# A five-layer attention stack on one core: the softmax shifts as eight rows per group, and who carries them

## What is computed

```
x = L0(x)                     # a0: cross attention on the normalised context
x = L1(x)                     # s1: self attention; c1: cross attention, raw context; m1: MLP
x = L2(x)                     # s2: self attention; c2: cross attention, normalised context; m2: MLP
x = L3(x)                     # l3: attention on the context with one wide head, experts, gate
attn = softmax(einsum('bhnd,bhsd->bhns', q, k) * HD ** -0.5)   # N = 256 queries, S = 1601 keys (or 256)
o = einsum('bhns,bhsd->bhnd', attn, v)
```

## Time and profile before

| what | value |
|---|---|
| median of the runs | 6120.44 us |
| the profiled execution: its own time | 6116.53 us |
| its span, first to last instruction | 6114.7 us |
| TensorE busy | 5496.7 us (90%) |
| ScalarE busy | 4374.0 us (72%) |
| VectorE busy | 4071.9 us (67%) |
| GpSimd busy | 990.6 us (16%) |
| mean granted TensorE clock | 0.976 |

### The profile page before, as it was taken

How to read it: one execution, slowest core, us unless ns; L and a number is a source line. 1 busy time by engine, 2 the same in 40 slices (tenths; PEclk the granted TensorE clock), 3 DMA queues, 4 the chain that set the end, 5 groups by cost and what they waited for, 6 DMA issues and landing times.

```text
span 6114.7 us, 229584 instructions
## 1 busy us (share of the span) xinstructions
PE 5496.7 (90%) x101728; PEld 3464.1 (57%) x101728; DVE 4071.9 (67%) x6107; ACT 4374.0 (72%) x8158; POOL 990.6 (16%) x1660
## 2 busy tenths in 40 slices
PE   5999999999877899999999977789999999998998
PEld 3555555656444466666666444446666666655665
DVE  5777777777555677777777445567777777744443
ACT  3888887888666688888888656568888888863333
POOL 3122122121111111111111011112211221200000
PEclk9999999999999899999999989989999999999999
DMA  2222222222112222222222011122222222211110
GB/s 94 83 78 60 85 75 61 87 74 59 49 56 65 86 74 74 78 85 75 77 74 82 2 58 58 59 86 81 64 78 87 75 65 85 75 44 33 46 59 27
DMA packets 230104, 414.47 MB, mean 68 GB/s; under 512 B 23904, under 2 KB 131472, under 8 KB 228624
## 3 DMA queue, kind: packets, MB, share of 16 engines
q1 hardware_dynamic: 229136, 400.04, 21.9%
HBM read 316.81 MB, written 83.14 MB: 65 GB/s over the span
## 4 chain that ended last, share of the span: by engine, by line
PE 66%; ACT 13%; DVE 9%; issue 5%; DMA 3%; POOL 2%; SPq 1%; ACTq 0%; DVEq 0%; POOLq 0%
PE bank L1158 25%; PE bank L1279 14%; PE pair L1158 14%; ACT P L1426 6%; DVE MX L1589 5%; ACT KSF L1396 2%; PE bank L758 2%; PE bank L749 1%; ACT QP L1364 1%; PE pair L685 1%; DMA QP<-scr_q 1%; PE bank L1195 1%; DMA scr_ks<-KSF 1%; ACT REST L1397 1%; PE pair L522 1%
## 5 line engine op out<-in xcount | busy, mean ns | idle before, releaser
L1589 DVE TENSOR_REDUCE MX<-pair 128x2 f32<-128x802 f32 x3072 | 2985.9, 990 | 1043.2 <-PE pair L1158 1030.6
L1426 ACT ACTIVATE P<-bank 128x512 f32<-128x512 f32 (+1 forms) x5504 | 3183.3, 597 | 606.3 <-PE bank L1158 497.6
L1158 PE MATMUL bank<-QP,KP 128*32 128x256 bf16 (+2 forms) x40192 | 2260.7, 274 | 223.7 <-ACT P L1426 169.7
L1158 PE MATMUL pair<-KP,QP 96*32 96x401 bf16 (+2 forms) x25264 | 1837.8, 335 | 152.9 <-DMA QP<-scr_q 98.9
L1158 PEld LDWEIGHTS bank<-QP,KP 128*32 128x32 bf16 (+2 forms) x40192 | 1109.0, 96 | 1356.6 <-ACT P L1426 345.3
L1279 PE MATMUL bank<-P,VA 128*25 128x256 f32 (+1 forms) x22016 | 1737.6, 383 | 0.5 <-ACT P L1426 0.5
L1158 PEld LDWEIGHTS pair<-KP,QP 96*32 96x32 bf16 (+1 forms) x25264 | 773.3, 97 | 297.6 <-DVE MX L1589 140.2
L1279 PEld LDWEIGHTS bank<-P,VA 128*25 128x25 f32 (+1 forms) x22016 | 641.3, 104 | 136.3 <-issue 47.1
L1718 POOL COPY VA<-VN 128x416 f32<-128x416 f32 (+1 forms) x320 | 139.7, 437 | 2745.8 <-PE bank L1279 1529.6
L1593 DVE TENSOR_REDUCE MX<-pair 128x4 f32<-128x1024 f32 x256 | 312.0, 1223 | 343.2 <-PE pair L1158 342.2
L1698 POOL TENSOR_TENSOR REST<-REST,KSF 128x401 f32<-128x401 f32 (+1 forms) x224 | 203.7, 910 | 538.0 <-ACT REST L1397 538.0
(11 more groups left out here) (245 smaller groups left out, 4235.7 us busy)
## 6 DMA issues: line engine op xcount, KB each, us to landing
KP<-scr_k SPq DMA_DIRECT2D x768, 225.1 KB
QP<-scr_q SPq DMA_DIRECT2D x960, 48.0 KB
CN<-ctx_n SPq DMA_DIRECT2D x40, 768.0 KB
scr_k<-KSF SPq DMA_DIRECT2D x48, 600.8 KB, 3.4
scr_k<-KSF SPq DMA_DIRECT2D x48, 600.0 KB, 3.3
CT<-ctx_t SPq DMA_DIRECT2D x24, 800.5 KB, 4.4
KP<-scr_ks SPq DMA_DIRECT2D x128, 144.0 KB
scr_q<-QS SPq DMA_DIRECT2D x80, 192.0 KB, 2.1
```

Of the source, the lines that this page charges most:

```text
L1158: last = nc.tensor.matmul(out[c:c + m, :], lhsT[:, c:c + m], rhs, start=start, stop=stop)
L1426: nc.scalar.activation(P[v % 2][0:kt, half * 2 * N:(half + 1) * 2 * N], SC[half][0:kt, :], ACT.Exp, scale=SCALE).then_inc(sem("probs_full" ...
L1589: nc.vector.tensor_reduce(MX[:, r, c:c + 2], MP[j % 2][:, :].rearrange("p (t k) -> p t k", t=2)[:, :, 0:SPANS[0][1]], AX.X, ALU.max).then_ ...
```

## The change

- **Rows.** NMB becomes 2 x 24 columns (query half, then 8 columns of shifts with zeros on both sides). `shifts` writes the 4 heads x (high, low) side by side. TensorE's 8 products become 2, each with 16 columns of weights (`row_products`): the result is 16 partitions x 256 queries, of which 8 carry one head's high and low each.
- **Ones per head.** Rows 96 to 111 of KP are one only in the columns of the head that a row belongs to, and zero elsewhere (`head_rows`). All four heads share the same 16 rows of QP.
- **Who copies.** VectorE copies the 16 x 256 to QP for the first head, waits for itself, and spreads it from SBUF to SBUF over the three others (16 x 768). ScalarE's two copies are gone. Both halves of tile 0's scores wait for the spread.
- **Self attentions.** The same from MP[1]; TensorE's `maximum` 1 of the next group waits for the copy (`rows_copied`), no longer for both of ScalarE's. Columns of MP are ordered by query half first.
- **Statistics.** `bn_aggr` of tile t - 1 stands behind `bn_stats` of tile t; the last slot has two.
- **Start.** VectorE's 2 memsets of rows become 32 (GpSimd's too); two small ones clear NMB.

```diff
+def head_rows():
+    cross, own = [(h, h * S, (h + 1) * S) for h in range(1, G)], [(h, h * N, (h + 1) * N) for h in range(G)]
+    return [[(2 * h + 2, c0, c1, 1.0) for h, c0, c1 in cross] + [(2, G * N, S, 1.0)] +
+            [(8 + 2 * h + 2, c0, c1, 1.0) for h, c0, c1 in own],
+            [(2 * h, c0, c1, 0.0) for h, c0, c1 in cross] + [(8 + 2 * h, c0, c1, 0.0) for h, c0, c1 in own],
+            [(2, 0, G * N, 1.0)]]
...
# tensor: piece "rows", and shift_rows with MP[1] and rows_full
-                    for half in range(2):
-                        for r in range(4):
-                            last = nc.tensor.matmul(MISC[ROWS_AT[half]:ROWS_AT[half] + 2, r * 128:(r + 1) * 128],
-                                                    NMB[g % 2][:, 4 * half + r, :], IDB[:, :], start=True, stop=True)
-                    last.then_inc(sem("misc_full"), 1)
+                    row_products(ph, g, MISC).then_inc(sem("misc_full"), 1)
...
+            def row_products(ph, g, out):
+                c = 8 if ph.cross else 0
+                for qt in range(2):
+                    last = nc.tensor.matmul(out[MR:MR + NR, qt * 128:(qt + 1) * 128], NMB[g % 2][:, qt, c:c + NR],
+                                            IDB[:, :], start=True, stop=True)
+                return last
...
# tensor: scores, t == 0
-                    use, pair = rows_at[ph.name, b, g]
-                    if use is not None and half:
-                        pe.wait_ge(sem("misc_free"), use + 1)
-                    else:
-                        pe.wait_ge(sem("rows_done"), pair + half + 1)
+                    pe.wait_ge(sem("rows_done"), rows_at[ph.name, b, g] + 1)
...
# tensor: maximum, j == 1
-                    pe.wait_ge(sem("rows_done"), rows_before(ph, b, g)[1] + 2)
+                    pe.wait_ge(sem("rows_copied"), rows_before(ph, b, g) + 1)
...
# scalar: piece "rows" (copy_rows in the self attentions goes alike)
-                    act.wait_ge(sem("misc_full"), el.use(role, "r" + name[-1]) + 1)
-                    nc.scalar.copy(QP[g][MR:MR + 2, half * 2 * N:(half + 1) * 2 * N],
-                                   MISC[ROWS_AT[half]:ROWS_AT[half] + 2, :]).then_inc(
-                        sem("misc_free" if half else "rows_done"), 1)
...
# vector: start
-            dve.wait_ge(sem("keys_cleared"), 1)
-            for g in range(2):
-                last = nc.vector.memset(KP[g][MR:MR + 2, :], 1.0)
-            last.then_inc(sem("packs_set"), 1)
+            for k, step in enumerate(head_rows()):
+                dve.wait_ge(sem("keys_cleared"), k + 1)
+                for g in range(2):
+                    for rows, c0, c1, value in step:
+                        last = nc.vector.memset(KP[g][MR:MR + rows, c0:c1], value)
+                last.then_inc(sem("keys_cleared"), 1)
...
# vector: rows
+            def spread_rows(g):
+                nc.vector.tensor_copy(QP[g][MR:MR + NR, N:G * N].rearrange("p (h q) -> p h q", q=N),
+                                      QP[g][MR:MR + NR, 0:N].unsqueeze(1).to_broadcast([NR, G - 1, N])).then_inc(
+                    sem("rows_done"), 1)
...
                 if role == "rows":
+                    use, g = el.use(role, name), el.group(int(name[1]) + 1)[2]
+                    dve.wait_ge(sem("misc_full"), use + 1)
+                    nc.vector.tensor_copy(QP[g][MR:MR + NR, 0:N], MISC[MR:MR + NR, 0:N]).then_inc(sem("misc_free"), 1)
+                    dve.wait_ge(sem("misc_free"), use + 1)
+                    spread_rows(g)
                     return
...
# vector: statistics
-                    wait_apart(dve, "stats_read", at("stats_read", b, t + 1))
-                    last = nc.vector.bn_aggr(MV[:, b, t, :], ST[:, t, :])
-                    if t == FULL:
-                        last.then_inc(sem("stats_done"), 1)
+                    for done in range(max(t - 1, 0), t + 1 if t == FULL else t):
+                        wait_apart(dve, "stats_read", at("stats_read", b, done + 1))
+                        last = nc.vector.bn_aggr(MV[:, b, done, :], ST[:, done, :])
+                        if done == FULL:
+                            last.then_inc(sem("stats_done"), 1)
```

More of the change, by code:

```diff
@@ L53 @@
 SHORT = ["mean", "var", "q", "k0", "k1", "k2", "k3", "d", "e", "y"]
-NO_BANK = ["square", "norm", "ctx_scale", "ctx_norm"] + STATS + ["low%d" % g for g in range(NG)]
+NO_BANK = ["square", "norm", "ctx_scale", "ctx_norm"] + STATS
 PHASES = ("a0", "s1", "c1", "m1", "s2", "c2", "m2", "l3")
@@ L326, in build @@
         ph.misc_after = misc
-    rows_at, full_at, pairs, full = {}, {}, 0, 0
+    rows_at, full_at, done, full = {}, {}, 0, 0
     for ph in plan:
@@ L336, in build @@
                     t_ph, t_b, t_g = el.group(g + 1)
-                    if ph.cross:
-                        rows_at[t_ph.name, t_b, t_g] = (el.use("rows", "r%d" % g), pairs)
-                        pairs += 1
-                    else:
-                        rows_at[t_ph.name, t_b, t_g] = (None, pairs)
+                    rows_at[t_ph.name, t_b, t_g] = done
+                    done += 1
+                    if not ph.cross:
                         full_at[t_ph.name, t_b, t_g] = full
-                        pairs, full = pairs + 2, full + 2
+                        full += 1
     def rows_before(ph, b, g):
         if g or b:
-            return rows_at[(ph.name, b, g - 1) if g else (ph.name, b - 1, NG - 1)]
-        return rows_at[ph.before.name, B - 1, NG - 1] if ph.before else None
+            return full_at.get((ph.name, b, g - 1) if g else (ph.name, b - 1, NG - 1))
+        return full_at.get((ph.before.name, B - 1, NG - 1)) if ph.before else None
     stream_total = {k: (ph.misc_after, ph.after().get("stream_done", 0) if not isinstance(ph, LastPhase) else 0)
@@ L404, in build @@
         NMF = sb("NMF", [128, 2 * G], f32)
-        NMB = [sb("NMB%d" % k, [128, 2 * G, 2], bf16) for k in range(2)]
+        NMB = [sb("NMB%d" % k, [128, 2, 24], bf16) for k in range(2)]
+        NMD = [NMB[k][:, :, 8:16].rearrange("p q (h i) -> p q h i", i=2) for k in range(2)]
         XMA = sb("XMA", [D, B * N], f32)
@@ L1242, in maximum @@
                     pe.wait_ge(sem("packed_loaded%d" % g), at("packed_loaded%d" % g, b, ph.c.per["packed_loaded%d" % g]))
-                elif j == 1 and rows_before(ph, b, g) and rows_before(ph, b, g)[0] is None:
-                    pe.wait_ge(sem("rows_done"), rows_before(ph, b, g)[1] + 2)
+                elif j == 1 and rows_before(ph, b, g) is not None:
+                    pe.wait_ge(sem("rows_copied"), rows_before(ph, b, g) + 1)
                 wait(pe, "max_done", at("max_done", b, g * ph.nm + j - 1))
@@ L1262, in shift_rows @@
                 pe.wait_ge(sem("shift_ready"), ph.c.at("shift_ready", b, g + 1))
-                for half in range(2):
-                    for r in range(4):
-                        c = half * 512 + r * 128
-                        last = nc.tensor.matmul(MP[1][MR:MR + 2, c:c + 128], NMB[g % 2][:, 4 * half + r, :],
-                                                IDB[:, :], start=True, stop=True)
-                    last.then_inc(sem("rows_full"), 1)
+                row_products(ph, g, MP[1]).then_inc(sem("rows_full"), 1)
             def head_values(ph, b, g, t):
@@ L1432, in copy_heads @@
                 nc.scalar.copy(RS[:, p * N:(p + 1) * N], OB[:, 0:N]).then_inc(sem("heads_copied"), 1)
-            def copy_rows(ph, b, g):
-                for half in range(2):
-                    act.wait_ge(sem("rows_full"), full_at[ph.name, b, g] + half + 1)
-                    nc.scalar.copy(QP[g][MR:MR + 2, half * 2 * N:(half + 1) * 2 * N],
-                                   MP[1][MR:MR + 2, half * 512:(half + 1) * 512]).then_inc(sem("rows_done"), 1)
             def element(el):
@@ L1455, in element @@
                             copy_heads(*el.prev, 1)
-                        if ahead and not ph.cross and t == ph.shift_tile:
-                            copy_rows(*ahead)
                         for piece_ in behind:
@@ L1488, in _ @@
             nc.vector.memset(VN[:, FULL, :], 0.0)
+            for k in range(2):
+                nc.vector.memset(NMB[k][:, :, :], 0.0)
             nc.vector.memset(OB[:, :], 0.0).then_inc(sem("cleared"), 1)
@@ L1611, in element @@
                 for g in range(NG):
+                    ahead = el.group(g + 1)
                     for t in range(ph.nt):
@@ L1624, in element @@
                             shifts(*mine[-1][:3])
+                        if ahead and not ph.cross and t == ph.shift_tile:
+                            copy_rows(*ahead)
                         for piece_ in (among if ph.cross else []) + behind:
@@ L1668, in _ @@
             pool.wait_ge(sem("packs_cleared"), 1)
-            for g in range(2, NG):
-                last = nc.gpsimd.memset(KP[g][MR:MR + 2, :], 1.0)
-            last.then_inc(sem("ones_set"), 1)
-            pool.wait_ge(sem("ones_set"), 1)
```

(6 more changed lines are left out.)

42 lines of the change are left out of this document (23 added, 19 removed).

## The result

| | before | after |
|---|---|---|
| median of the runs | 6119.6 us (6113.71 to 6120.67, 4 runs) | 5957.39 us (5953.76 to 5961.58, 4 runs) |
| ratio, 95% interval | | 0.9737, 0.972 to 0.9754 |
| profiled execution | 6116.5 us, span 6114.7 | 5956.5 us, span 5954.7 |
| predicted | | 5925 us, range 5865 to 6040 |

The change makes the kernel 2.6% faster, and the median lies in the range. The gain is 162 us where 195 were forecast.

The account below looks back on a forecast made before the run. ScalarE's two row copies were taken to be on the path at 190 cross-attention borders, and VectorE to bound a0's statistics groups. -86.6 - 108.8 - 12.8 + 13.0 = -195.2 from 6116.5 gives 5921.3, forecast as 5925 us, range 5865 to 6040.

Parts of the forecast that it names:

- a0: First cross-attention phase: 2.98 us per element from borders and 2.6 from statistics, 86.6 us saved in all.
- c1 and c2: The two cross-attention phases without statistics: 3.43 us saved per element at the borders, 108.8 us in all.
- self attentions: 0.4 us saved in each of 32 elements, 12.8 us, with between +25 and -30 us allowed.
- start: Memsets on VectorE add 15.6 us before the first projection, the first element's statistics return 2.6: +13.0 us.
- The spread: VectorE's 768-column bfloat16 copy within SBUF at each border, taken as 0.36 us, upper bound 0.96.
- the first rival: The spread takes 0.55 us, so late borders lose 0.19 us more each: 5963 us in all; chance 0.15.
- The copy: VectorE's copy of 256 columns from PSUM at each border, taken as 0.41 us, bounds 0.3 and 0.5.
- The fewer products: TensorE's 6 saved products per border, counted at nothing, at most 0.1 us each.
- Border 3→0: Border into the next element, VectorE the tighter engine: 0.05 us gained in a0, 0.5 in c1 and c2.
- The statistics: `bn_aggr` one token behind saves 0.22 us for 12 of 13 tokens, 2.6 us an element, or 1.5.
- the rows are ready 0.1 us later than they were: Self attentions: scores at 1704.66 instead of 1704.55, with 0.81 us until the rows are there.
- VectorE the bound behind each border: VectorE's added work pushes out tile 1's reductions, half of the borders' 156 us is lost: 6003; chance 0.17.

Follow-up runs that it names:

- rows alone: The changed kernel with the statistics put back in their old order: 6005.71 us (0.9811).
- even form: The changed kernel with the spread walked as 2 x 3 x 128 instead of 3 x 256 onto one run of 768: 5935.14 us (0.9696).
- second spread: The changed kernel with one more spread, into an unused buffer, ahead of the real one: 6096.04 us; with the rows' piece one slot earlier too: 6062.4 us.
- earlier rows: The changed kernel with the rows' piece of the cross attentions one slot earlier (t = 10 instead of 11): 5941.71 us (0.9706).
- the even form and hardly any collisions: The changed kernel with the spread as 2 x 3 x 128, except at one border per cross element where GpSimd subtracts: 5917.8 us (0.9671).
- delayed fast copies: The changed kernel with 24 unneeded bfloat16 copies in eight forms in VectorE's idle time at the start: 5955.24 us in one run.
- VectorE's ones set later: The changed kernel with VectorE's memsets of KP[0] and KP[1] moved behind the first element's statistics: 5942.33 us (0.9708).

## Why the prediction was right, and which of its terms were not

The mechanism was right in the main: ScalarE's two copies were on the path at the cross borders, TensorE's waits for its first scores were their trace, 0.65 us for half 0 and, unseen by the prediction, up to 0.85 for half 1, and VectorE's copy and spread took their place. Of the 195 us, 160 came. Term by term, predicted and measured:

| term | predicted | measured |
|---|---|---|
| a0 | -86.6 | -75.9 |
| c1 and c2 | -108.8 | -91.2 |
| self attentions | -12.8 | +3.3 |
| start | +13.0 | +10.4 |
| behind the last shifts | 0 | -6.5 |

- **The spread.** This is the term that was mis-sized. RDX, a float32 source, was scaled by bytes to 0.36 us; measured 0.549. "By columns", 0.55, had the length right, and so had the first rival, which put the time at 5963 with it; 5957 was measured. With 0.549 in the prediction's own working for the borders where the rows come late, borders 0→1, 1→2 and 2→3 of a0 give 0.59, 1.08 and 0.76 us; measured 0.61, 1.07 and 0.80.
- **The copy**: 0.41 predicted, 0.430 measured.
- **The fewer products** were counted at nothing. They end 0.12 us sooner behind the first load than the eight did, and TensorE is free 0.22 us sooner, so it waits that much longer for late rows: 0.94 us where 0.42 of lateness was forecast. TensorE's busy time in the page fell by 126 us; it is modelled and holds more than work, so it doesn't say what the products are worth. No run changes the products alone: how the 115 us of the rows divide between ScalarE's copies and TensorE's products is open.
- **Border 3→0.** In a0 +0.05 was counted and -0.55 measured (rows alone); in c1 and c2 0.5 against 0.34 and 0.30. That VectorE is the tighter engine there was read rightly from the earlier trace rows, but then a small gain was still booked. Over the whole group the added 0.98 us took some 0.5 us from VectorE's idle time, and 0.55 made the group longer.
- **The statistics** were put at 2.6 us per element, or 1.5 if TensorE takes over. Alone they give 2.62, beside the rows 3.07, since there VectorE is even tighter. The chain is 0.26 us per token now, from 0.53 in the earlier trace rows:

```profile
50.66 0.26 DVE L1557 BATCH_NORM_STATS2 ST<-CN 128x6 f32<-128x128 f32 x1
50.84 0.17 DVE L1560 BATCH_NORM_AGGREGATE MV<-ST 128x2 f32<-128x6 f32 x1
50.92 0.26 DVE L1557 BATCH_NORM_STATS2 ST<-CN 128x6 f32<-128x128 f32 x1
```

- **Self attentions.** A gain of 12.8 us was forecast, a loss of 3.3 came. One trace says little of 3 us here: in those with this same code s1 and s2 take 960.4 to 971.6 us together (961.0 before), and the longer ones have the lower clock (s2: 483 us at 0.89, 495 at 0.86). What is shown is that the gain did not come. The step that failed is "the rows are ready 0.1 us later than they were". From the first row product to the first scores it is 1.38 us now:

```profile
1657.69 0.28 PE L1173 MATMUL pair<-IDB,NMB 128*16 128x128 bf16 x2 [0.34 <-DVE NMB L1619]
1658.00 0.43 DVE L1525 CAST QP<-pair 16x256 bf16<-16x256 f32 x1 [0.37 <-PE pair L1173]
...
1658.47 0.55 DVE L1517 COPY QP<-QP 16x768 bf16<-16x768 bf16 x1
...
1659.07 0.39 PE L1166 MATMUL bank<-QP,KP 128*128 128x256 bf16 x2 [1.11 <-DVE QP L1517]
```

  Before it was 1.05 (first product at 1703.50 in that trace, scores at 1704.55): 0.33 us more, of which 0.11 was forecast, 0.19 is the spread and 0.02 the copy. Two of the four borders (0→1, 2→3) still win 0.35 to 0.63 us, the other two lose 0.45 to 0.75. The gain at the border with piece d was seen; that 3→0 could lose although a load is waited for there was not. With the even form s1 and s2 together take 950.5 to 953.2 us in four traces, 8 to 11 less than before.
- **Start.** The first projection was forecast near 46 us and stands at 44.74: 13.8 us of memsets instead of 15.6. The statistics gave back 3.4 instead of 2.6.
- **Behind the last shifts** 6.5 us were saved that no term had. The kernel with the statistics alone doesn't have them (710.6 us there), those with the rows on VectorE do (700.2 to 702.6). They lie at one place of l3: before, ScalarE stands 5.00 us ahead of an exponential with no wait that the profile shows, and from 5610 to 5620 us TensorE's granted clock is 0.68.

```profile
5614.36 0.66 ACT L812 ACTIVATE P<-bank 128x256 f32<-128x256 f32 x2 [5.00 <-issue]
```

  The kernel with the statistics alone has the same hold (5.10 us), the change has none there. What holds ScalarE is open.
- **VectorE the bound behind each border** was a rival with 0.17, and priced as the loss of half the gain (6003). As a price that was too high; as a description it was right, if VectorE's work at the border is meant and not its load. The changed kernel already is there: the same second spread costs the cross borders nearly as much with the rows early as with them late. My expectation of 52 to 72 us from earlier rows rested on the opposite.
- **The sum of the errors** is 28 us in the cross attentions and 16 in the self attentions. With the even form and hardly any collisions, which is nearly the spread as it was priced, 39.6 us come back: the cross attentions then give 192.4 us where 195.4 were forecast, the self attentions 9.6 where 12.8 were. Most of both hangs on 0.19 us of one instruction.
- **Luck.** In a0 the statistics gave 0.47 us an element more than counted, which hides most of the 0.60 by which border 3→0 was wrong, and the 6.5 us behind the last shifts came from no term. The median lies in the range, but above the 5870 to 5945 us that the prediction gave its own forecast: it is the first rival's 5963 that came.

## What to carry to other kernels

When work moves to an engine that is 75% busy, price it at the place where others wait for that engine: here each 0.47 us more in front of the rows cost 0.46 us a border, though VectorE was idle for some us in the same group. A new operation's length wants a row of the same form, not only of the same kind; where there is none, a few copies in idle time at the start tell it. And if a faster form of an instruction gives much less than its length says, look at the maximum beside the median, and at what the other engines do in the slow ones.

## What the runs showed of the hardware

- On VectorE the same 768 bfloat16 columns, SBUF to SBUF, took 549 ns as 3 repeats of 256 into one run, 356 as 2 x 3 x 128 (median) and 356 as a plain run with GpSimd idle; 1,024 columns as 4 repeats took 423. 16 or 128 partitions made 4 ns of difference.
- The faster form and GpSimd's subtraction or scaling on SBUF shut each other out; the slower form doesn't. Beside GpSimd's 0.9 us subtraction the 356 ns became about 0.91 us, in 45 spreads of 320, and they mostly ended about 0.2 us after it. The slower form met the same subtraction 46 times and stayed at 548 to 551 ns. It goes the other way too: GpSimd's scaling of CN took 448 ns alone and 539 to 546 in the four that ran beside the delayed fast copies (the second line has these four and two of 448). The Trainium skill (SBUF — State Buffer, Who interferes with whom) calls the shared port pair an exclusive lock; the spreads agree with that.

```profile
L1723 POOL TENSOR_SCALAR CN<-CN,CR,CO 128x128 f32<-128x128 f32 x4 | 1.7, 448 | 0.4 <-DVE CO L1571 0.4
...
L1723 POOL TENSOR_SCALAR CN<-CN,CR,CO 128x128 f32<-128x128 f32 x6 | 3.0, 510 | 0.0
```

- TensorE's mean granted clock in s2 was 0.89 in the change and 0.81 with the second spread, which holds the rows back by 0.47 us more at each border.

The best version found is the change with the even form, the rows a tile earlier and VectorE's ones set later: 5885.94 us, 3.9% less than before and 1.2% less than the change.
